# A causal attention layer: squares to ScalarE, weight scaling and splitting to GpSimd, the output tile ahead of the query projection

## The reference

```python
xn = layernorm(x)
q = xn @ wq                            # per head: 128 columns without, 64 with rotation
ckv, k_pe = split(xn @ wkv_a)          # 128 latent columns, 64 rotated ones
ckv = ckv * rsqrt(mean(ckv**2) + 1e-6) * kv_norm_scale
k_nope, v = split(ckv @ wkv_b)         # per head 128 and 128
scores = (q_nope @ k_nope.T + rope(q_pe) @ rope(k_pe).T) * 192**-0.5   # causal
out = softmax(scores) @ v              # then, over all heads, @ wo
result = x + out @ wo + (sum_r xn @ factors[r]) / sqrt(8) + bias
```

## Time and profile before

| | us |
|---|---|
| median of 3 runs | 1648.32 (1648.1 to 1649.82) |
| the profiled execution | 1651.71 |
| its span, first to last instruction | 1649.8 |
| TensorE busy | 1536.0 (93%) |
| VectorE busy | 1044.7 (63%) |
| ScalarE busy | 931.6 (56%) |
| GpSimd busy | 892.6 (54%) |
| mean granted clock of TensorE | 0.976 of full speed |

### The profile page before, as it was taken

How to read it: one execution, slowest core, us unless ns; L and a number is a source line. 1 busy time by engine, 2 the same in 40 slices (tenths; PEclk the granted TensorE clock), 3 DMA queues, 4 the chain that set the end, 5 groups by cost and what they waited for, 6 DMA issues and landing times.

```text
span 1649.8 us, 25138 instructions
## 1 busy us (share of the span) xinstructions
PE 1536.0 (93%) x7876; PEld 823.9 (50%) x7876; DVE 1044.7 (63%) x2416; ACT 931.6 (56%) x2261; POOL 892.6 (54%) x857
## 2 busy tenths in 40 slices
PE   5669898989898989999999999999999999999997
PEld 4534454545454545445454554554555555555554
DVE  8765566657666666555555556556656666676877
ACT  6534555655565655665656666666555566544554
POOL 2655554545454645555655566565745556554553
PEclk9879999999999999999999999999999999999999
DMA  8725676757676859867777677687867776864654
GB/s 256 246 44 127 140 147 128 143 126 157 128 152 134 159 113 184 172 137 165 149 162 155 142 149 144 137 190 140 184 137 154 143 146 156 177 148 105 139 137 125
DMA packets 646883, 246.68 MB, mean 150 GB/s; under 512 B 599392, under 2 KB 612192, under 8 KB 646112
## 3 DMA queue, kind: packets, MB, share of 16 engines
q1 hardware_dynamic: 646752, 245.08, 69.3%
HBM read 79.30 MB, written 23.07 MB: 62 GB/s over the span
## 4 chain that ended last, share of the span: by engine, by line
PE 66%; DVE 15%; ACT 10%; issue 6%; POOL 2%; DMA 1%; SPq 0%; ACTq 0%; DVEq 0%; POOLq 0%
PE ps L345 13%; PE ps L347 13%; PE ps L346 13%; ACT ex L666 6%; PE ps L480 5%; PE ps L485 5%; PE ps L486 5%; PE ps L482 5%; PE ps L481 5%; DVE gm L984 3%; DVE ps L986 2%; DVE acc L1029 2%; DVE nm L1002 1%; ACT st L676 1%; DVE sqr L779 1%
## 5 line engine op out<-in xcount | busy, mean ns | idle before, releaser
L1172 POOL TENSOR_TENSOR st<-ex,st 128x512 f16<-128x512 f32 (+3 forms) x640 | 645.7, 1025 | 663.0 <-ACT st L676 650.9
L666 ACT ACTIVATE ex<-ps,nm,scales 128x512 f32<-128x512 f32 (+3 forms) x640 | 452.1, 709 | 640.9 <-DVE nm L1002 640.9
L676 ACT ACTIVATE st<-ex 128x512 f16<-128x512 f32 (+3 forms) x640 | 342.2, 561 | 6.1 <-ACT ex L666 0.4
L984 DVE TENSOR_REDUCE gm<-ps 128x1 f32<-128x512 f32 (+1 forms) x384 | 248.8, 667 | 117.5 <-PE ps L486 115.4
L480 PE MATMUL ps<-kTh,q 128*128 128x512 f16 (+3 forms) x640 | 225.0, 352 | 24.5 <-ACT ex L666 19.7
L485 PE MATMUL ps<-kRh,q 128*128 128x512 f16 (+3 forms) x640 | 223.6, 349 | 9.1 <-POOL q L1163 8.9
L345 PE MATMUL ps<-pT,vH 128*128 128x512 f16 (+3 forms) x640 | 228.6, 357 | 0.0
L346 PE MATMUL ps<-pT,vH 128*128 128x512 f16 (+3 forms) x640 | 226.4, 354 | 0.0
L482 PE MATMUL ps<-kTh,q 128*128 128x512 f16 (+3 forms) x640 | 223.5, 349 | 0.0
L481 PE MATMUL ps<-kTl,q 128*128 128x512 f16 (+3 forms) x640 | 223.5, 349 | 0.0
L486 PE MATMUL ps<-kRl,q 128*128 128x512 f16 (+3 forms) x640 | 223.4, 349 | 0.0
(11 more groups left out here) (181 smaller groups left out, 2320.8 us busy)
## 6 DMA issues: line engine op xcount, KB each, us to landing
wV<-w_vo SPq DMA_DIRECT2D x48, 512.0 KB, 3.6
wA<-w_abs SPq DMA_DIRECT2D x48, 256.0 KB, 3.0
pT<-st SPq DMA_TRANSPOSE x640, 3.2
early<-factors_in SPq DMA_DIRECT2D x32, 256.0 KB, 3.8
w_vo<-wV SPq DMA_DIRECT2D x16, 512.0 KB, 3.0
wP<-w_pe SPq DMA_DIRECT2D x24, 256.0 KB, 3.1
wsq<-wq_in SPq DMA_DIRECT2D x16, 256.0 KB, 3.4
wso<-wo_in SPq DMA_DIRECT2D x16, 256.0 KB, 2.8
```

Of the source, the lines that this page charges most:

```text
L666: e.activation(ex[:, n % NEX, 0:keys], s_bank(n)[:, 0:keys], ACT.Exp, bias=nm[:, (i * QT + r) % 4:(i * QT + r) % 4 + 1], scale=scales[:, p ...
L676: e.activation(stage(n, keys)[:, :, 0, :], ex[:, n % NEX, 0:keys].rearrange("p (t n) -> p t n", n=P), ACT.Copy).then_inc(z["a_pH"], 1)
L984: e.tensor_reduce(m, b, AX_X, ALU.max).then_inc(z["v_max"], 1)
L1172: e.tensor_tensor(s[:, :, 1, :], ex[:, n % NEX, 0:keys].rearrange("p (t n) -> p t n", n=P), s[:, :, 0, :], ALU.subtract).then_inc(z["g_pL" ...
```

## The change

- **Squares.** VectorE's `squares`, `latent_squares` and `factor_squares` go. ScalarE sums squares with an activation (Square, with accumulation), one 512-column block each: `sqp` in row block 1 of odd units, `sq0` in block 2, `sq1` in block 3, for the pair prepared two units later; `sqk` (256 columns) in block 0 of the even unit, `sqf` in unit 0, block 0. In the start-up they stand at t = 2, 3, 16 and 17.
- **GpSimd** scales the keys' and values' weights (`sk`, `sv`, block 3 of the unit before) and splits wo (`wo_low`, block 1, behind `parts`). In the start-up, scale_keys(0) stands behind the first four factor additions.
- **Order.** `out` stands ahead of `q` in row block 0 of all units; `tkv` moves from block 1 to block 0; `parts` moves from block 1 to block 0 in the last chunk.
- **The scale** uses another bound: the sum of the query squares times a fourth root of a power of the keys' row sums, so VectorE gets a few operations on one column (`row_powers`, `fourth_root`).
- **SP** issues the second pair's loads in the middle of the factor loads, and some semaphores are now kept for each buffer.

The core of the diff:

```diff
@@ fills @@
     if r == 0:
         if 1 <= i <= H:
             out.append(("wo", i - 1))
-        if i + 1 < NU:
-            out.append(("q", i + 1))
-        if 3 <= i + 2 <= H + 2:
-            out.append(("sv", i + 2))
-        if i % 2 == 0 and i + 2 < H:
-            out.append(("sq", i + 2))
-        if i == 0:
-            out.append(("sqf", 0))
     if i == NU - 1:
         out += [("out", (i - 2) * QT + t) for t in range(QT) if r == 3]
     elif 2 <= i:
         out.append(("out", (i - 2) * QT + r))
+    if r == 0:
+        if i + 1 < NU:
+            out.append(("q", i + 1))
+        if i + 2 <= H + 2:
+            out.append(("tkv", i + 2))
+        if i % 2 == 0 and i + 2 < H:
+            out += [("sqk", i + 2), ("r8", i + 2)]
+        if i == 0:
+            out.append(("sqf", 0))
+        if i // H == NC - 1 and i + 1 < NU and (i + 1) % H:
+            out.append(("parts", i + 1))
...
+        if i + 2 < H:
+            out.append(("tq", i + 2))
+        if 1 <= i <= NU:
+            out.append(("den", i - 1))
+        if i // H < NC - 1 and i + 1 < NU and (i + 1) % H:
+            out.append(("parts", i + 1))
         if 1 <= i <= H:
             out.append(("wo_low", i - 1))
-        if i + 2 < H:
-            out.append(("tq", i + 2))
-        if i + 2 <= H + 2:
-            out.append(("tkv", i + 2))
-        if 1 <= i <= NU:
-            out.append(("den", i - 1))
-        if i + 1 < NU and (i + 1) % H:
-            out.append(("parts", i + 1))
+        if i % 2 and i + 3 < H:
+            out.append(("sqp", i + 3))
...
+        if i % 2 and i + 3 < H:
+            out.append(("sq0", i + 3))
+    if r == 3:
+        if i % 2 and i + 3 < H:
+            out += [("sk", i + 3), ("sq1", i + 3)]
+        if 4 <= i + 3 <= H + 2:
+            out.append(("sv", i + 3))
@@ TensorE @@
-                e.wait_ge(z["v_wo"], h + 1)
+                e.wait_ge(z["g_wo"], h + 1)
@@ ScalarE @@
+            def square_sum(w, at, total):
+                return e.activation(sqr[:, at:at + w.shape[-1]], w, ACT.Square, accum_out=total)
...
+                e.wait_ge(z[load], loads * (i // 2 + 1))
...
+                square_sum(w, at, total).then_inc(z["a_" + kind], 1)
@@ ScalarE, loop over t @@
+                if t == 2:
+
+                    e.wait_ge(z["a_sqa"], 1)
+                    squares("sqk", 0)
+                    squares("sq0", 0)
+                if t == 3:
+                    squares("sq1", 0)
+                    squares("sqp", 0)
...
+                if t == NT:
+                    squares("sq0", 2)
+                    squares("sq1", 2)
+                if t == NT + 1:
+                    squares("sqp", 2)
@@ GpSimd @@
+            def scale_keys(i):
+
+                e.wait_ge(z["d_scl"], 16)
+                for n in range(2):
+                    e.wait_ge(z[f"d_wk{n}"], 16 * (i // 2 + 1))
+                w = wsk[:, :, :].rearrange("p a n -> p (a n)")
+                e.tensor_tensor(w, w, scl[:, 0:1].broadcast_to([P, 2 * P]), ALU.mult).then_inc(z["g_sk"], 1)
...
+            def w_o(h):
+                e.wait_ge(z["a_wo"], h + 1)
+                e.tensor_tensor(wV[:, h % 2, 1, :], wso[:, :], f(wV[:, h % 2, 0, :]), ALU.subtract).then_inc(
+                    z["g_wo"], 1)
...
             for i in range(NF):
                 factor(i)
+                if i == KE + 3:
+                    scale_keys(0)
+            scale_keys(2)
+            scale_values(3)
@@ SP @@
-            e.wait_ge(z["g_fac"], NF - KE)
+                if n == 4:
+                    for m in range(2, 4):
+                        load_wk(m)
+                        load_wq(m)
+                    load_wp(2)
+                    load_wv(3)
             load_wo(0)
```

More of the change, by code:

```diff
@@ L380, in norm @@
                 b = free_bank(key)
-                e.wait_ge(z[ready], count(key))
+                for name in ready:
+                    e.wait_ge(z[name], count(key))
                 e.matmul(b[:, 0:columns.shape[-1]], ones[:, :], columns, start=True, stop=True).then_inc(
@@ L630, in transpose_x, with squares, factor_squares @@
                 e.activation(x_tile(t, 0), by4(bank(("xt", t))), ACT.Copy).then_inc(z["a_xt"], 1)
+            def square_sum(w, at, total):
+                return e.activation(sqr[:, at:at + w.shape[-1]], w, ACT.Square, accum_out=total)
+            def squares(kind, i):
+                w, at, total, load, loads = {
+                    "sqp": (wsp[:, :, :].rearrange("p k n -> p (k n)"), 0, nrm[:, 2:3], "d_wp", 64),
+                    "sq0": (wsq[:, 0, :, :].rearrange("p k n -> p (k n)"), E, nrm[:, 0:1], "d_wq0", 16),
+                    "sq1": (wsq[:, 1, :, :].rearrange("p k n -> p (k n)"), 2 * E, nrm[:, 1:2], "d_wq1", 16),
+                    "sqk": (wsk[:, :, :].rearrange("p a n -> p (a n)"), 3 * E, rows[:, 0:1], "g_sk", 1)}[kind]
+                e.wait_ge(z[load], loads * (i // 2 + 1))
+                if i:
+                    e.wait_ge(z["p_nrm"], i // 2)
+                    e.wait_ge(z["a_" + kind], i // 2)
+                if i and kind == "sqk":
+                    e.wait_ge(z["v_r4"], i // 2)
+                square_sum(w, at, total).then_inc(z["a_" + kind], 1)
+            def factor_squares():
+                e.wait_ge(z["g_fac"], NF - KE)
+                for kind in ("sqp", "sq0", "sq1", "sqk"):
+                    e.wait_ge(z["a_" + kind], 2)
+                square_sum(fsum.rearrange("p k n -> p (k n)"), 0, nrf[:, :]).then_inc(z["a_sqf"], 1)
             def w_pe(i):
@@ L698, in fill @@
                     factors_high()
+                elif kind in ("sqp", "sq0", "sq1", "sqk"):
+                    squares(kind, n)
+                elif kind == "sqf":
+                    factor_squares()
             def factors_high():
@@ L792, in squares, with row_powers @@
+            def row_powers(i):
+                e.wait_ge(z["a_sqk"], i // 2 + 1)
                 if i:
                     e.wait_ge(z["p_nrm"], i // 2)
[L794 to L799, removed]
@@ L800, in squares @@
-                square_sum(wsk[:, :, :].rearrange("p a n -> p (a n)"), 3 * E, 2 * P, nrm[:, 2:3]).then_inc(z["v_sq"], 1)
+                    e.wait_ge(z["v_r8"], i // 2)
+                e.tensor_tensor(rows[:, 1:2], rows[:, 0:1], rows[:, 0:1], ALU.mult).then_inc(z["v_r4"], 1)
+                e.wait_ge(z["v_r4"], i // 2 + 1)
+                e.tensor_tensor(nrm[:, 3:4], rows[:, 1:2], rows[:, 1:2], ALU.mult).then_inc(z["v_r8"], 1)
             def scale_pair(i):
                 t, sc = tot[:, i // 2, :], scales[:, i // 2, :]
+                b = bank(("nrm", i))
@@ L1051, in fill @@
                     w_abs(n)
-                elif kind == "wo_low":
-                    w_o(n)
                 elif kind == "wpe_low":
@@ L1188, in _ @@
                 factor(i)
+                if i == KE + 3:
+                    scale_keys(0)
+            scale_keys(2)
+            scale_values(3)
             q_rope(0)
             rope_parts(0)
-            for i in range(NU):
+            for i in range(NU + 1):
                 for r in range(QT):
-                    for p in range(chunk(i) + 1):
-                        low_parts(i, r, p)
+                    if i < NU:
+                        for p in range(chunk(i) + 1):
+                            low_parts(i, r, p)
                     for kind, n in fills(i, r):
-                        if kind == "pe":
+                        if kind == "sk":
+                            scale_keys(n)
+                        elif kind == "sv":
+                            scale_values(n)
+                        elif kind == "wo_low":
+                            w_o(n)
+                        elif kind == "pe":
                             q_rope(n)
```

139 lines of the change are left out of this document (60 added, 79 removed).

## The result

The changed kernel takes 1705.62 us (median of 4 runs, 1705.11 to 1707.01) against 1649.07 (1648.1 to 1650.03) for the kernel before on the same chip: ratio 1.034, 95% interval 1.033 to 1.036. Forecast were 1669 and a range of 1632 to 1692: the sign was right, and the loss 56.6 us where 21 were forecast. The profiled execution has a span of 1703.7 us and a mean clock of 0.979 (0.976 before).

What follows compares the result with a forecast made beforehand. TensorE was taken to set the time, held by VectorE in the first chunk's even units. Start +9.5, first chunk -26.2, later chunks +4.9, +16 and +16.8 gave +21.0 us: 1669 us as runs' median, range 1632 to 1692.

Steps and rivals of the forecast that it cites:

- +16: Units 32 to 47: output ahead of query projection waits bare for oT, 2.0 us in each of 8 pairs.
- +16.8: Units 48 to 63: bare output wait and VectorE's chain cost +2.1 us in each of 8 pairs.
- +9.5: Start: ScalarE waits for GpSimd's key scaling behind four factor additions, delaying VectorE's first latent step; 7 to 11 us.
- so nothing absorbs the delay: Start: VectorE works without a break from the first latent step to 60 us, so the +9.5 us stays.
- -26.2: First chunk: 7.6 us gained in each of six even units, less 1.5 (even) or 1.7 (odd) for late w_o.
- free the fourth bank just in time, so none of it is given back: First chunk, even units: exponentials starting at 273.5 cause no new TensorE wait, keeping the 7.6 us gain.
- L1015 at 11.75: Last chunk, unit without rope: VectorE's step finishing oT comes 11.75 us after the previous one, 11.46 before.
- B: Rival: output wait hidden, as ScalarE and VectorE reach oT before TensorE's scores end; 1625 us, chance 0.16.
- D: Rival: TensorE at 1.2 GHz after waits, 1.7 us lost per pair of last two chunks; +27, 1696 us, chance 0.08.
- C: Rival: w_o costs nothing in the first chunk, GpSimd being done before w_vo; 1644 us, chance 0.12.
- F: Rival: the start is not delayed; 1660 us, chance 0.05.
- E: Rival: table loads of 1.28 us around each Square among the exponentials; +36, 1705 us, chance 0.04.

Runs made afterwards that it cites:

- out_behind_q: Changed kernel with the output product put back behind the query projection in row block 0 of every unit: 1660.13 us, ratio 1.006.
- before_out_ahead: Kernel before, with only the output product moved ahead of the query projection in row block 0: 1717.42 us, ratio 1.041.
- two_fixes_behind: Changed kernel with scale_keys(0) ahead of the factor additions, w_o ahead of rope_parts, and output behind the query projection everywhere: 1622.07 us, ratio 0.984.
- covered_wait: Changed kernel with unused filler matmuls ahead of the output's wait for oT from unit 32 on: 1688.81 us, ratio 1.024.
- rope_parts_back: Changed kernel with output ahead only up to unit 17 and the last chunk's rope parts back in row block 1: 1639.45 us, ratio 0.994.
- three_fixes_parts_back: Changed kernel: output ahead only up to unit 17, scale_keys(0) before factor additions, w_o before rope_parts, last chunk's parts in block 1: 1600.77 us, ratio 0.970.
- wo_first: Changed kernel with GpSimd's w_o ahead of rope_parts in row block 1: 1679.70 us, 25.9 less than the changed kernel.
- keys_first: Changed kernel with GpSimd's scale_keys(0) ahead of the factor additions: 1697.87 us, 7.8 less than the changed kernel.

## Why the prediction was wrong

In short: the waits that the prediction named were there, the output's at nearly the length forecast, and the sign came from them. Two steps of its sum failed by most of the difference. The +16 and +16.8 price the output wait alone and take the clock behind it at nothing, where 11 stretches at half clock cost 18.6 us; and they take the waits and VectorE's chain too short, by 11 us.

**The start, +6.3 for +9.5.** The chain held to about a microsecond: GpSimd's additions, key scaling to 24.6 (24.8 forecast), ScalarE idle 8.2 us, the sum at 28.33 (28.8; before 19.51), the first latent step at 32.46 (33.6; before 24.10). The step that failed is "so nothing absorbs the delay": it looked no further than 60 us. The seventh latent step is still 8.8 us late; before the last one VectorE waited 4.95 us for ScalarE, and coming late it waits 1.87. The kernel before, then the changed one:

```profile
79.30 0.17 DVE L923 RECIPROCAL ssq<-ssq 128x2 f32<-128x2 f32 x1 [4.95 <-ACT ssq L601]
...
85.61 0.17 DVE L955 RECIPROCAL ssq<-ssq 128x2 f32<-128x2 f32 x1 [1.87 <-ACT ssq L614]
```

**First chunk, -20.1 for -26.2.** L382 and L372 are gone from TensorE's waits, and w_vo waits 1.27 us in odd and 1.70 in even units, where 1.7 and 1.5 were forecast. Regular pairs take 75.3 us for 74.5. The missing part is in the even unit, -4.8 to -5.1 for -6.1. There the step failed that the exponentials "free the fourth bank just in time, so none of it is given back": ScalarE starts them 5.65 us behind its copy of q and not 5.3, and the second wait below, 0.46 us, is new. The first, 0.76, had been 0.59 before, and the forecast had allowed 0.5 more. w_vo takes 0.2 more, and the rest of the even unit's loss I did not locate:

```profile
271.51 0.28 PE L493 MATMUL ps<-kTh,q 128*128 128x256 f16 x1 [0.76 <-ACT ex L703]
...
280.83 0.34 PE L493 MATMUL ps<-kTh,q 128*128 128x384 f16 x1 [0.46 <-ACT ex L703]
```

The regular pairs miss 4.2 us in all. The first pair, from q of unit 2 to q of unit 4, gained 0.6 and the sixth 1.5 (with a stretch at half clock behind w_vo), 6.7 less than the forecast's 4.4 each; units 13 to 17 paid 0.9 for 5.5, so 4.6 came back by a second miss, which is luck.

And the gain was put down to one part too many. I named the early output tile among what frees VectorE but gave it no price, and counted the output's move as a cost of 0.2; out_behind_q and before_out_ahead show that either part alone leaves the pair at 78.3 to 78.5, and only both together give 75.3. That holds while w_o is late: with w_o in time, two_fixes_behind has 73.2 without the early output, so there the work taken off VectorE is worth 5.3 us a pair and the early output 1.3.

**Units 18 to 31, +5.1 for +4.9.** Right: pairs of 51.77 for 51.03, +0.74.

**Units 32 to 47, +29.9 for +16.** The wait was right: 1.89 us for 1.8, and at the other change of units 0.37 from the last score's start to the output's, 0.3 above its step of 0.07 before, as forecast. The steps that failed are the clock, taken at nothing in the forecast, 5 stretches of 1.7 us = 8.5, and the size of the rest: a pair without such a stretch takes 38.46 us, 2.5 more than before and not 2.0. The first pair of the chunk pays more, 3.6 us in covered_wait, where no stretch is left (49.28 for 45.66).

**Units 48 to the end, +32.8 for +16.8.** Six stretches at half clock are about 10. Without one a pair is 26.29 us (12.48 + 13.81), +2.85 for +2.1: the term "L1015 at 11.75" in the chain of the unit without rope. Its steps hold up to the maxima of block 1 (5.60 us behind oT, 5.6 forecast); block 2 comes at 7.59 for 7.2 and block 3 at 9.34 for 8.6, so oT at 12.48. What is longer are the biases (L1035) of blocks 1 and 2:

```profile
1573.91 0.69 DVE L1048 TENSOR_TENSOR oT<-ps,oT 128x512 fp32r<-128x512 f32 x1 [0.17 <-ACT oT L720]
...
1579.51 0.42 DVE L1019 CUSTOM_DVE_ANT_0 ps<-ps,cmask 128x256 f32<-128x256 f32 x1
...
1580.03 0.61 DVE L1035 SCALAR_TENSOR_TENSOR nm<-gm,scales,head 128x1 f32<-128x1 f32 x1
...
1581.50 0.54 DVE L1019 CUSTOM_DVE_ANT_0 ps<-ps,cmask 128x384 f32<-128x384 f32 x1
...
1582.13 0.54 DVE L1035 SCALAR_TENSOR_TENSOR nm<-gm,scales,head 128x1 f32<-128x1 f32 x1
...
1583.25 0.68 DVE L1019 CUSTOM_DVE_ANT_0 ps<-ps,cmask 128x512 f32<-128x512 f32 x1
...
1584.03 0.22 DVE L1035 SCALAR_TENSOR_TENSOR nm<-gm,scales,head 128x1 f32<-128x1 f32 x1
```

They take 0.61 and 0.54 us where the one of block 3 takes 0.22, in 12 of the 13 stretches from one oT to the next between 1493 and 1682 us; that is 0.7 of the 0.73 us by which oT is later than forecast. Why they are longer stays open; in the kernel before it was those of blocks 2 and 3, with 0.47 and 1.15 (from 1570 us). The 0.56 to 0.9 us of L485's wait did vanish, but rope_parts_back and three_fixes_parts_back show that this gains nothing and costs some 2 us by q of unit 62. That the unit is paced by VectorE's chain, and not by that wait, fits this and is argued.

**The rivals.** B fell: the output wait is bare in both kernels that have the order. D was right in kind: covered_wait puts it at 17 us (I gave 27 if every pair loses, and every pair does not). My reason against it, that the last chunk had idle time at full clock, compared waits of 0.56 to 0.9 us in that chunk's pairs with one of 1.9 to 2.4 us, which I had just forecast myself. C fell to wo_first and F to keys_first, which show both costs. E fell, though its 1705 us is the time that was measured, by chance:

```profile
L703 ACT ACT_TABLE_LOAD x1 | 1.3, 1283 | 0.0
```

This and the first are the only loads of the changed kernel, with 26 squares behind the first exponential. The Trainium skill (ScalarE: Activation LUTs, "Table sets: the hidden batching unit") lets functions of one set follow each other without a load, and on this chip Square and Exp do.

**Accounting.** By the spans the change costs 53.9 us, 33 beyond the forecast: 18.6 are the clock (11 stretches of 1.7), 6.1 the first chunk's smaller gain, -3.2 the start, and the remaining 11 the sizes of the output waits and of VectorE's chain in the last two chunks.

## What to carry to other kernels

Work that waits for the end of a chain belongs behind work that does not, above all where the order is written out once and applied to stages of different length: the same line gained 3 us a pair in the long units of the first chunk (1.3 once w_o was in time) and lost 0.7 to 4.5 a pair in the shorter ones, and a condition on the stage made the change a small gain, 0.4%. When a kernel that has TensorE busy 100% gets a new bare wait, price the clock with it: here the 28 waits of over a microsecond behind 1130 us cost 18.6 us more, 0.7 each on average. A change of several parts may hold small mistakes of queue order (one key scaling behind four additions, one split behind two rope parts) that are worth more than the idea; reading each new instruction's place in its engine's queue found both before the run, and moving them, with the output behind from unit 18 on, made a slower kernel 2.7 to 3.0% faster than the start.

## What the runs showed of the hardware

Behind 1130 us TensorE waited over a microsecond in 28 places, and fell to 1.2 GHz in 11 of them. Of the 16 waits of 1.9 to 3.3 us ten were followed by slow matmuls, with equal waits in equal units: those that ended at 1262.54 and 1302.67 were, that of 1342.81 was not. Of the eight of 1.2 us only one was followed by them, that ending at 1463.34, 1.5 us after the end of another wait, of 1.6. So short waits were safer here, but which of the long ones fall could not be read from their length. That matmuls whose results nobody uses prevent every one of them, and make the kernel 1% faster, I had not expected. The Trainium skill (TensorE: Matmul & The Clock Gate, "HAM oscillation — how this bites in real kernels") tells of kernels that fall back to half clock in every round of a loop; this trace agrees in part: the fall comes again and again, at 1.7 us each, but not in every round.
